# An adaptive-norm and mixture-of-experts kernel on one core: the order of the first transfers

## The reference

```python
# L0_cond: hidden 512, common factors of rank 16 and expert factors of rank 16, ALPHA = 2
hidden_i = x @ wi.T + ALPHA * (x @ common_wi_a.T) @ common_wi_b.T + expert_lora(x, expert_ids)
hidden_i = relu(hidden_i)
hidden_o = hidden_i @ wo.T + ALPHA * (...) + expert_lora(hidden_i, expert_ids)
# L0_ffn: 4 rounds of a mixture of 4 experts, the 2 best of each token, softmax over the two
for r in range(4):
    w = softmax(top2(cur @ Wg[r] + bg[r]))
    cur = cur + sum_e w_e * (gelu(cur @ W1[e] + b1[e]) @ W2[e] + b2[e])
x = x + cur
# L1_cond: a factor pair and an embedding of the batch's language, then L1_ffn:
h = silu(z @ w1 * s1) * (z @ w2 * s2)
h = gelu(h @ h1 * s); h = gelu(h @ h2 * s)
x = x + h @ w3 * s3
```

## Time and profile before

| | |
|---|---|
| median of 3 runs | 484.82 us (484.8 to 484.99) |
| the profiled execution's own time | 486.61 us |
| its span | 484.8 us |
| PE busy | 477.9 us, 99% of the span |
| PEld busy | 397.0 us |
| DVE busy | 387.7 us |
| ACT busy | 393.9 us |
| POOL busy | 118.7 us |
| the chain that ended last | PE 96%, DMA 2%, SPq 1% |

### The profile page before, as it was taken

One profiled execution on the slowest core, in us unless ns is written; L12 is line 12 of the kernel. 1 busy time (PEld: TensorE's weight loads), 2 busy tenths in 40 slices (PEclk: granted clock), 3 DMA queues, 4 the chain that ended last, 5 costly groups with the idle time before them and its releaser, 6 DMA issues.

```text
span 484.8 us, 7478 instructions
## 1 busy us (share of the span) xinstructions
PE 477.9 (99%) x2270; PEld 397.0 (82%) x2270; DVE 387.7 (80%) x641; ACT 393.9 (81%) x542; POOL 118.7 (24%) x102
## 2 busy tenths in 40 slices
PE   7999999999999999999999999999999999999997
PEld 7998888888888888888888888888888887888885
DVE  4789899999879898988898898889897758554343
ACT  3799988888888888988888888888888888697653
POOL 5796212121212112121222121231313144400000
PEclk9999999999999999999999999999999999999999
DMA  7702702020201102020202012120202000000001
GB/s 209 215 5 88 266 18 89 2 87 3 87 11 76 71 16 87 0 87 0 87 0 87 11 76 82 49 89 0 87 2 87 2 0 0 1 0 1 0 22 69
DMA packets 6986, 26.30 MB, mean 54 GB/s; under 512 B 2226, under 2 KB 2610, under 8 KB 4786
## 3 DMA queue, kind: packets, MB, share of 16 engines
q1 hardware_dynamic: 5826, 21.20, 12.1%
q0 software_dynamic: 528, 3.67, 2.2%
q10 hardware_dynamic: 608, 1.11, 0.8%
HBM read 24.81 MB, written 1.18 MB: 54 GB/s over the span
## 4 chain that ended last, share of the span: by engine, by line
PE 96%; DMA 2%; SPq 1%; issue 0%; DVE 0%
PE bank L505 34%; PE bank L506 34%; PE bank L509 26%; DMA stage<-lora_all 2%; PE bank L594 1%; PE bank L595 1%; PE bank L527 1%; SPq L244 0%; SPq L247 0%; PE bank L540 0%; PE bank L524 0%; SPq L257 0%; DVE x L1276 0%; SPq L345 0%; SPq L344 0%
## 5 line engine op out<-in xcount | busy, mean ns | idle before, releaser
L812 ACT ACTIVATE act_out<-bank,vec 128x512 f32<-128x512 f32 x256 | 165.4, 682 | 41.8 <-PE bank L509 32.6
L1115 DVE TENSOR_TENSOR hid_lo<-act_out,hid_hi 128x1024 fp32r<-128x1024 f32 x128 | 156.6, 1243 | 33.3 <-ACT hid_hi L817 33.2
L817 ACT ACTIVATE hid_hi<-act_out 128x1024 fp32r<-128x1024 f32 x128 | 135.9, 1062 | 8.0 <-PE bank L509 0.2
L468 POOL TENSOR_TENSOR cur<-cur,prod 128x512 f32<-128x512 f32 x48 | 64.9, 1352 | 238.4 <-DVE prod L1126 237.9
L505 PE MATMUL bank<-hid_hi,moe_hi 128*128 128x512 f32 x256 | 99.9, 390 | 0.0
L509 PE MATMUL bank<-hid_hi,moe_lo 128*128 128x512 f32 x256 | 99.7, 390 | 0.0
L505 PE MATMUL bank<-xhi,moe_hi 128*128 128x512 f32 x256 | 99.7, 390 | 0.0
L506 PE MATMUL bank<-hid_lo,moe_hi 128*128 128x512 f32 x256 | 99.7, 389 | 0.0
L506 PE MATMUL bank<-xlo,moe_hi 128*128 128x512 f32 x256 | 99.6, 389 | 0.0
L509 PE MATMUL bank<-xhi,moe_lo 128*128 128x512 f32 x256 | 99.6, 389 | 0.0
L505 PEld LDWEIGHTS bank<-hid_hi,moe_hi 128*128 128x128 f32 x256 | 48.1, 188 | 11.3 <-issue 0.2
(11 more groups left out here) (126 smaller groups left out, 569.9 us busy)
## 6 DMA issues: line engine op xcount, KB each, us to landing
cw_all<-cw_dram SPq DMA_DIRECT2D x16, 1024.0 KB, 4.6
stage<-ffn_w POOLq DMA_DIRECT2D x1, 2304.0 KB, 8.5
cw_all<-moe_w SPq DMA_DIRECT2D x4, 512.0 KB, 10.3
stage<-lora_all SPq DMA_DIRECT2D x5, 160.0 KB, 7.1
x<-x_t POOLq DMA_DIRECT2D x3, 256.0 KB, 7.0
out_t<-x SPq DMA_DIRECT2D x3, 256.0 KB, 2.5
cur<-cond_base ACTq DMA_DIRECT2D x2, 256.0 KB, 3.1
stage<-ffn_w POOLq DMA_DIRECT2D x1, 512.0 KB, 3.8
```

Source lines behind the costliest of these rows:

```text
L468: pool.tensor_tensor(cur[:, c, :], cur[:, c, :], prod[:, s % 2, :], ALU.add).then_inc(add_done, 1)
L812: act.activation(act_out[:, f // 2, f % 2, :], bank[:, f, :], ACT.Gelu_apprx_tanh, bias=vec[:, V_B1 + e * FC + f:V_B1 + e * FC + f + 1]).t ...
L817: act.activation(hid_hi[:, s % 2, 2 * pr:2 * pr + 2, :], act_out[:, pr, :, :], ACT.Copy)\
L1115: dve.tensor_tensor(hid_lo[:, s % 2, 2 * pr:2 * pr + 2, :], act_out[:, pr, :, :], hid_hi[:, s % 2, 2 * pr:2 * pr + 2, :].bitcast(F32), ALU ...
```

## The change

GpSimd's three transfers of x wait for batch 3's factors instead of the second half of batch 1's. On ScalarE's queue batch 3's factors go ahead of base's second part. SyncE no longer waits for base's first part before batch 2's factors.

```diff
@@ sync
             first_load(sp, 0)
-            expert = lora_expert(sp, 2)
-            sp.wait_ge(base_in[0], 16)
-            expert_load(sp, 2, expert)
-            for b in (4, 5, 6, 7):
+            for b in (2, 4, 5, 6, 7):
                 lora_load(sp, b)
@@ gpsimd
-            pool.wait_ge(first_out_in[1], 16)
+            pool.wait_ge(lora_in[3], 16)
             for c in range(1, CHUNKS):
                 x_load(pool, c)
@@ scalar
             first_load(act, 1)
+            lora_load(act, 3)
             base_load(act, 1)
-            lora_load(act, 3)
             x0_high(0)
```

## The result

| | before | after |
|---|---|---|
| median | 485.03 us (484.67 to 485.76, 11 runs) | 487.04 us (484.94 to 490.31, 11 runs) |
| profiled execution, own time | 486.61 us | 488.77 us |
| its span | 484.8 us | 487.0 us |

The ratio is 1.0047, interval 1.0027 to 1.0067: slower, by 2.0 us in the medians. The changed kernel also scatters five times as far as the one before (5.4 us from lowest to highest, against 1.1). The profiled execution is of the second group.

A forecast was written before the change was run, and what follows sets the result against it. It took the start, ahead of 18.4 us, to hold the winnable time: late batch 5 factors and x chunk 1. With chunk 1 landing at 12.8, 1.2 us came off the 484.82 us median, giving 483.6 us, range 482.4 to 485.3.

The forecast's parts named there:

- SyncE's wait: On SyncE ahead of batch 2's factors: base's first part had already come at 3.6, so removing the wait gives 0.
- Batch 3's factors: On ScalarE's queue, ahead of base's second part: issued at 4.56, landing at 7.4 (bounds 6.7 and 9.0) instead of 9.4.
- Base: Base's second part on ScalarE's queue: issued at 5.17, 1.34 us later, landing at 8.9 instead of 7.3.
- Chunk 1: Second 256 KB of x on GpSimd's queue: 5.4 us to land, at 12.8 against 12.65 before (bounds 10.6 and 14.2).
- So base costs nothing on the path while it lands by about 10.3: On DVE: with base at 8.9, the last sum of batches 2 and 3 ends at 13.1, no later than 13.14 before.
- seven steps of 0.60 us: DVE's work from base's landing to the last sum of batches 2 and 3, batch 0's low half included: 4.2 us.
- Nothing waits.: GpSimd's three x issues hold it 1.94 us, to 9.3; its first low half ends at about 10.9, delaying nothing.
- Batch 0's output product at L + 2.9 = 15.7, batch 2's at L + 4.5 = 17.3: Two chains from x chunk 1's landing L, through ScalarE and GpSimd: starts earlier by 1.3 and 1.2 us.
- The sum: Saving 14.0 - L, L being x chunk 1's landing, capped at 2.4 us: 1.2 us off the 484.82 median, 483.6 us.
- Nothing to tell: Rival, 30%: factors early only as x is late; L of 13.3 to 14.5 saves 0.7 to -0.5, about 484.5 us.
- Slower by x: Rival, 10%: chunk 1 still takes 6.8 us, L is 15.0, ScalarE's copy holds batch 0's relu: 485.8 us.
- Slower by the clock: Rival, 5%: earlier merges leave a TensorE gap at about 14.2 to 15.7, where the clock falls: 485.3 us or more.

The follow-up runs named there:

- e4: Kernel before with only SyncE's wait ahead of batch 2's factors removed: 485.29 us, ratio 1.0000.
- e8: The changed kernel run again unaltered, for its spread: 488.05 us (484.76 to 490.78, 12 runs), ratio 1.0048; its profile fell on a run of the lower group.
- e3: Kernel before with only GpSimd's x transfers made to wait for batch 3's factors: 487.95 us, ratio 1.0053.
- e5: Changed kernel with DVE's first low half moved ahead of the sum that waits for base's second part: 485.31 us, ratio 1.0000.
- e6: Changed kernel with 8 warming matmuls between merge group 3 and batch 0's products: 486.71 us, ratio 1.0027.
- e2: Kernel before with only ScalarE's two transfers swapped, batch 3's factors ahead of base's second part: 486.16 us, ratio 1.0012.
- e7: Kernel before with DVE's first low half one place later, behind the sum of batch 1's second matrix: 485.63 us, ratio 1.0013.
- e11: Changed kernel with 20 warming matmuls instead of 13 ahead of the first merges: 486.29 us, ratio 1.0025.
- e12: Kernel before with 20 warming matmuls instead of 13: 486.06 us, ratio 1.0024.
- e9: Changed kernel with DVE's low half ahead of base's sum and, on ScalarE, batch 0's relu ahead of x chunk 1's copy: 485.82 us, ratio 1.0008.
- e10: Kernel before with ScalarE's two transfers swapped and DVE's low half ahead of base's sum: 484.82 us, ratio 0.9991.

## Why the prediction was wrong

It said 483.6 us, 482.4 to 485.3; measured were 487.04. Two steps failed: that a late base costs nothing, and the reference from which the saving was counted. Its steps in order:

- **SyncE's wait is worth 0**: right (e4, 1.0000).
- **Batch 3's factors**, issued 4.56 and landed 7.4: measured 4.50 and 7.4. **Base**, issued 5.17 and landed 8.9: 5.11 and 8.9. **x**, issued at 7.4: 7.72. **Chunk 1** after 5.4 us, at 12.8: 5.4 us, at 13.1. Every transfer was priced right, to 0.3 us.
- **"So base costs nothing on the path while it lands by about 10.3"**: this is the step that failed, and the loss comes from it. Its seven steps of 0.60 us priced the low half wherever it stood. Moved from 8.71, ahead of GpSimd's subtract, to 9.56, beside two of them, it took 3.16, and TensorE needs it for its very next products; it stood still for 3.16 us. The base transfer landed inside the forecast's bound and the time was still lost. The rows that could have warned stood in the timeline of GpSimd of the kernel before, between those of the earlier trace rows:

```profile
8.94 1.57 POOL L417 TENSOR_TENSOR ffn_lo<-prod,ffn_hi 128x512 fp32r<-128x512 f32 x1 [1.12 <-ACT ffn_hi L798]
10.48 1.28 POOL L417 TENSOR_TENSOR ffn_lo<-stage,ffn_hi 128x512 fp32r<-128x512 f32 x1
```

  The first began 0.23 us behind DVE's low half and took 0.29 us more than the second. The two engines already met there, and the change turned around who waits for whom.
- **GpSimd's three issues: "Nothing waits."** Nothing waited for GpSimd. But the issues moved its subtracts from 8.94 onto 9.68, which is where DVE's had gone.
- **Batch 0's output product at L + 2.9 = 15.7, batch 2's at L + 4.5 = 17.3**: in a run without the hold (e8) 15.94 and 17.58, with L at 13.0; held, 19.35 and 20.87. The two chains are right wherever x is the last to come: e3 (L = 14.4) has 17.29 and 18.90, e5 (L = 12.1) 15.02 and 16.62.
- **The sum, 1.2 us off the median**: a second error, which would have stood without the hold. "The saving is 14.0 - L" counts from the 18.53 of the earlier trace rows, and these are of a profiled execution whose clock was at 0.50 from 11.08. That execution took 1.79 us more than the median, and what made it longer lies ahead of the mark: its clock, and batch 5's factors, which came at 15.76, when TensorE had been through with cond_hidden(1) since 15.37 even at the low clock. In e4 the same merges began at 14.81, and 17.44 stands for the 18.53. How the two share in it is not shown. (The difference between own time and span explains nothing here; it is about 1.8 us in every run.) An estimate for the median run, from its 485.03 us less the 468.2 that lie behind the mark on average in the 14 traces, is 16.8. The prediction's own chains, with L at 12.8, give 17.3, so no saving at all. A saving worked out on such a run must not be taken off the median. e5 shows what was left: 0 (0.9988 to 1.0011).
- **The rivals.** Nothing to tell: its mechanism, the factors early by as much as x is late, is what the runs without the hold show (e8 against e4), though at L = 13.0 and not at its 13.3 to 14.5. Slower by x: the direction is borne out by e3, 1.0053 at L = 14.4, though the price was far too low, and in the change L was 13.1. Slower by the clock: the right kind, since a new gap did cost the clock, and e6 puts 2.2 us of the loss on it; but it was put at 14.2 to 15.7 and came at 9.6 to 12.8. The hold that made the gap was on no list.

The Trainium skill, SBUF — State Buffer, in the section on who interferes with whom, says that a DVE instruction with two operands in SBUF and a GpSimd instruction that reads SBUF contend, and that the one which starts first keeps the other out for its whole length. The rows agree in kind (0.68 alone, 1.44 and 1.45 behind one subtract in e2 and e7). They don't agree in the 3.16 and 2.88 us: there DVE, blocked by one, stayed out for the next as well.

## What to carry to other kernels

Before a transfer is moved, ask which vector instructions it shifts in time and which other engine will then be reading SBUF beside them; an instruction whose own row grows beside another engine's (1.57 us here where its neighbour has 1.28) is the sign that two already meet. Order such instructions by program order where one of them is awaited by TensorE: here `first_low` ahead of the sum that waits for the late transfer healed all of it (485.31 against 485.29 us). And check that the profiled execution is an ordinary run, by its own time and its clock, before a saving worked out on it is taken off a median.

## What was not expected of the hardware

- Held by GpSimd, DVE's 0.68 us took 3.16 and 2.88 us over two subtracts in a row, and 1.44 and 1.45 over one. In the long ones the input of GpSimd's second subtract was there well before its first ended (ScalarE's copy done at 10.31, the first subtract at 10.95); in the short ones it came only about then (10.41 and 10.55 in e2), and DVE got in between. This reading fits four traces; no run tried it by itself. Another fits them as well: in the long ones the two rows began within 0.2 us of each other, in the short ones GpSimd's 0.4 us ahead. In all four DVE's row ends 0.55 or 0.56 us behind the end of the subtract that kept it out.
- DVE's row in the changed kernel begins 0.12 us ahead of GpSimd's (9.56 and 9.68), and DVE was the one held. With a lead of 0.23 (before, e4, e8, e11, e12) it never was; there GpSimd's first subtract took 1.57 to 1.61 us instead of 1.28.
- GpSimd's three issues of transfers (1.95 us from 7.49 in e5) lay beside DVE's two-operand subtract at 9.10 and didn't hold it: 0.69 us. In e9 the subtract (9.58, 0.69 us) lay wholly inside them (8.27 to 10.21).
- The same 26 records of warming matmuls took from 4.64 (e10) to 5.92 us (e4, e8, e9), with a granted clock of 1.00 in the records. The records themselves show two paces: about 9 to the us at first and 14 later. The step lies at about 4.5 us in the kernel before, 5 in the changed one and 6.5 in e8, and what sets it is open. The profiles fit the view that this decides into which group a run of the changed kernel falls (held with 4.89 us of warming, and with 4.98 in e6; not held with 5.92), and e11 supports it; it is not shown run by run.
- On GpSimd's queue x chunk 1 took 5.4 us for 256 KB in the changed kernel, with 61% of the engines' span in its queue in the window from 9.2 to 12 us, and 6.8 before; ScalarE's 256 KB at the start took 2.8 to 3.2. Size alone tells little of a transfer's time here.
